# Layer 0 of a three-layer interaction network rebuilt from squared pair sums, with the state copies on ScalarE and the products' tiles in 8 KB packets

## The chip, the cores and the metric

One core of a Trainium2 chip. The metric is the device time of one execution in microseconds, lower is better. Five engines work side by side and wait for one another through semaphores: TensorE (PE; its weight loads are PEld), VectorE (DVE), ScalarE (ACT), GpSimd (POOL) and SyncE (SP), which here only issues transfers. Sixteen DMA engines carry the transfers of all of them.

## The reference

For 1024 samples, 32 embedding rows of 16 numbers are gathered from 32 tables, and three layers of products of pairs follow, each with 64 outputs; the sums over the 16 numbers, with 16 context features, go through a small network.

```python
e = stack([tbl_f[ids[:, f]] for f in range(32)], axis=1)     # B=1024, M=32, D=16
x0 = xk = e
for W in (W0, W1, W2):                                        # W: M x H x 64, H = 32, 64, 64
    xk = relu(einsum('bmd,bhd,mhk->bkd', x0, xk, W))
    outs.append(sum(xk, axis=2))
h = concatenate([concatenate(outs, 1), dense_ctx], 1)         # 208 wide
h = maximum(h @ W_top1 + b_top1, 0)                           # 512
h = maximum(h @ W_top2 + b_top2, 0)                           # 256
y = h @ W_top3
```

Everything is float32. Layer 0 multiplies the embeddings with themselves, so it is symmetric in its two factors: 528 different products of rows. Layers 1 and 2 have 32 x 64 = 2048 products each for every one of the 16384 columns (sample and position).

## The kernel before

The 16384 columns are worked off in 16 **pairs** p of 1024 columns (two chunks of 512, which go to the lower and the upper 64 partitions of an accumulator). For a pair:

- GpSimd gathers 16 x 128 rows of 64 bytes (`gather`, L377) into `gath`, in the order that `stage` copies from the row numbers. SP stores them to a scratch tensor in DRAM (`store_x0`, L251), twice over, so that a row index can wrap.
- SP loads from the scratch what layer 0 needs (`load_x`, L255 to L262): `x_rep`, every row on all four blocks of 32 partitions, `x_rot`, the same rows turned by q + 4u, and `x16`, the turn by 16. Each of these transfers writes 32 partitions.
- SP loads the tiles `m_rep` (`load_m`, L271), 8 tiles of 128 x 1024: block q of tile t holds row 4t + q on all its 32 partitions. Four transfers of 1 MB, each writing 32 partitions. There are three buffers of 8 tiles.
- Layer 0: VectorE multiplies `x_rot` by `x_rep` (`layer0`, 2 units of two tiles, L455) and `x16` (L463); TensorE multiplies by the weights (L662, L674) into `acc0`.
- Layers 1 and 2: ScalarE applies the ReLU while it copies an accumulator four times (`order0`, L560) and eight times (`order1`, L568) into `rep0` and `rep1` (PSUM) and eight times into `xb_pool` (SBUF), and once more into `state` (L555). VectorE makes 6 units a layer (`layer`, L455, a unit is two tiles, `m_rep` times `rep`), GpSimd makes 2 (`products`, L416), of whose last VectorE makes a strip of 112 columns (`edge`). TensorE adds each unit with 4 matmuls of 512 columns (8 instructions, L662).
- VectorE sums each `state` over the 16 positions (`sum_d`, L471).

The order of a pair in the loops, on every engine, is layer 1 of p, layer 0 of p + 1, layer 2 of p - 1. Products go through a ring of 4 buffers (`RING`), with `unit_ready` and `unit_used`. `load_x(p + 2)` waits until VectorE has made layer 0 of p + 1 (`unit_ready`, `p16_ready`). Pair 0 is done in halves ahead of the loops (L508, L704, L582). After the last pair the sums are brought together by 12 transfers and the network at the end runs on TensorE and ScalarE (L760 to L777).

Of the kernel before, what the change touches and what calls it, by code (L numbers as in the profile page):

```python
# [7 lines left out]
U32 = mybir.dt.uint32  # L29
ALU = mybir.AluOpType  # L30
RELU = mybir.ActivationFunctionType.Relu
AX_X = mybir.AxisListType.X
# [6 lines left out]
HC = CHUNK // 2  # L39
NP = B * D // PAIR  # L40
BC = CHUNK // D
GPP = 2 * BC // Q
HG = GPP // 2
LEAD = 4
T = M // Q
DVE_UNITS = 6
POOL_UNITS = 2
RING = 4
M_BUFS = 3
EDGE = 112  # L50
L0_UNITS = 2
PER_ITER = 2 * DVE_UNITS + L0_UNITS
# [4 lines left out]
def build(nc, ids, limits, tables, wa, wb, w1, w2, wt1, bt1, wt2, bt2, wt3, dense, out):  # L57
    ctx = ExitStack()
    with ctx:
# [6 lines left out]
        def sem(name):  # L66
# [3 lines left out]

        x0_dram = nc.dram_tensor("x0_scratch", [NP, 2 * M, PAIR], F32).ap()

# [3 lines left out]
        row_now = [sb(f"row_now{i}", [128, GPP], U32) for i in range(2)]  # L76
        gath = [sb(f"gath{i}", [128, GPP, D]) for i in range(2)]

        x_rep = sb("x_rep", [128, PAIR])
        x_rot = sb("x_rot", [128, 4, PAIR])  # L80
        x16 = sb("x16", [2 * M, 2, CHUNK])

        m_rep = sb("m_rep", [128, M_BUFS * T, PAIR])
        wa_sb = sb("wa_sb", [128, 5, K])
        wb_sb = sb("wb_sb", [128, 4, K])
        w0_sb = sb("w0_sb", [128, 4, K])
# [28 lines left out]
        w0_in = sem("w0_in")  # L115
        w1_in = sem("w1_in")
# [5 lines left out]
        rows_staged = sem("rows_staged")  # L122
# [718 lines left out]
```

## Time and profile before

| | us |
|---|---|
| median of three runs | 773.81 |
| lowest, highest | 772.15, 776.86 |
| span of the profiled execution, first to last instruction | 775.5 |
| busy PE, DVE, POOL, ACT | 593.1, 595.6, 576.2, 408.5 |
| mean granted clock of TensorE | 0.921 of full |
| DMA: bytes, mean rate | 123.07 MB, 159 GB/s |

The page lists no time of the profiled execution other than its span, which lies within the three runs and 1.7 us above their median. Busy times overlap, so they do not add up to the span. No engine is above 77%: who waits for whom has to be read from the waits and from stretches of the timeline. [...]

### The profile page before, as it was taken

To read this page: it belongs to the slowest core of one execution; us is meant where nothing else is said; L and a number is where in the kernel's file an instruction comes from. 1 tells how busy PE (TensorE), PEld (TensorE's weight loads), DVE (VectorE), ACT (ScalarE), POOL (GpSimd) and SP (SyncE) were. 2 spreads that over 40 slices of the span, in tenths; PEclk is the share of its full clock that TensorE was granted. 3 is DMA by queue.
4 is the path that set the end of the run, shared out by engine and by line. 5 is a ranking of instruction groups with operands and counts; after the bars stand their busy time and mean duration, and the time that the engine had idled before them with its cause. 6 is when DMAs were issued, how large, how long until landed. Compare 5 with 4: busy or idle time off the path is not lost.

```text
span 775.5 us, 8340 instructions
## 1 busy us (share of the span) xinstructions
PE 593.1 (76%) x2532; PEld 189.3 (24%) x2532; DVE 595.6 (77%) x325; ACT 408.5 (53%) x724; POOL 576.2 (74%) x340
## 2 busy tenths in 40 slices
PE   0256563998289978969499959769599959799998
PEld 0133111322023222213123212213132212222243
DVE  0143459999399969879799958799899969899910
ACT  0123480867238673746357745727367726657522
POOL 6775679698868889898868888898978887626400
PEclk9968795999779998989799999999899989999999
DMA  3799989794979789797979698897979697990000
GB/s 88 160 195 210 204 180 202 156 206 91 204 147 208 151 170 203 152 205 151 204 150 205 118 201 173 182 199 155 205 152 204 136 207 151 203 197 8 7 8 0
DMA packets 56099, 123.07 MB, mean 159 GB/s; under 512 B 16177, under 2 KB 25265, under 8 KB 56082
## 3 DMA queue, kind: packets, MB, share of 16 engines
q1 hardware_dynamic: 47890, 120.75, 76.8%
q0 software_dynamic: 8192, 2.11, 3.0%
q8 instruction: 8, 0.13, 0.1%
q14 instruction: 9, 0.07, 0.0%
HBM read 117.84 MB, written 4.20 MB: 157 GB/s over the span
## 4 chain that ended last, share of the span: by engine, by line
POOL 27%; DVE 18%; issue 16%; DMA 15%; PE 14%; ACT 5%; SPq 4%; POOLq 0%; DVEq 0%; ACTq 0%
DVE prod L455 16%; POOL gath L377 16%; POOL prod_pool L416 11%; PE acc L662 10%; DMA x<-x_scratch 8%; DMA gath<-in_tables,row_now 4%; ACT rep L568 4%; PE rep L769 2%; DMA x_scratch<-gath 2%; SPq L251 1%; DMA m_rep<-x_scratch 1%; DVE z_sb L471 1%; SPq L258 1%; SPq L255 1%; PE rep L760 1%
## 5 line engine op out<-in xcount | busy, mean ns | idle before, releaser
L662 PE MATMUL acc<-prod,w_sb 128*64 128x512 f32 x1728 | 425.2, 631 | 119.2 <-DVE prod L455 117.9
L455 DVE TENSOR_TENSOR prod<-m_rep,rep 128x2048 f32<-128x2048 f32 x186 | 416.1, 2273 | 17.9 <-DMA m_rep<-x_scratch 10.1
L377 POOL DMA_INDIRECT gath<-in_tables,row_now x256 | 287.1, 1121 | 81.8 <-issue 68.4
L416 POOL TENSOR_TENSOR prod_pool<-m_rep,xb_pool 128x2048 f32<-128x2048 f32 (+1 forms) x62 | 276.7, 4490 | 62.0 <-PE acc L662 54.6
L568 ACT ACTIVATE xb_pool<-acc 32x512 f32<-32x512 f32 x248 | 146.0, 589 | 162.4 <-PE acc L674 157.6
L662 PEld LDWEIGHTS acc<-prod,w_sb 128*64 128x64 f32 x1728 | 124.0, 144 | 407.4 <-issue 230.1
L568 ACT ACTIVATE rep<-acc 32x512 f32<-32x512 f32 x248 | 139.9, 564 | 68.4 <-DVE prod L455 63.4
L455 DVE TENSOR_TENSOR prod<-x_rot,x_rep 128x2048 f32<-128x2048 f32 x30 | 101.9, 3436 | 75.8 <-DMA x<-x_scratch 72.2
L662 PE MATMUL acc<-prod_pool,w_sb 128*64 128x512 f32 x496 | 117.2, 593 | 4.5 <-POOL prod_pool L416 4.5
L560 ACT ACTIVATE rep<-acc 64x512 f32<-64x512 f32 x124 | 70.7, 570 | 51.2 <-DVE prod L455 25.6
L704 PE MATMUL acc<-prod,w_sb 128*64 128x256 f32 x128 | 21.5, 498 | 48.5 <-DVE prod L508 48.4
L662 PEld LDWEIGHTS acc<-prod_pool,w_sb 128*64 128x64 f32 x496 | 35.4, 137 | 76.9 <-issue 71.0
L471 DVE TENSOR_REDUCE z_sb<-state 128x512 f32 (+1 forms) x48 | 32.3, 673 | 6.2 <-ACT state L555 6.2
L555 ACT ACTIVATE state<-acc 128x512 f32<-128x512 f32 x47 | 26.5, 596 | 14.3 <-PE acc L662 13.5
L582 ACT ACTIVATE rep<-acc 32x256 f32<-32x256 f32 (+1 forms) x24 | 8.5, 353 | 47.2 <-PE acc L724 46.9
L508 DVE TENSOR_TENSOR prod<-m_rep,rep 128x2048 f32<-128x2048 f32 x6 | 13.5, 2283 | 20.2 <-DMA m_rep<-x_scratch 18.5
L463 DVE TENSOR_TENSOR prod<-x 64x512 f32<-64x512 f32 x15 | 27.0, 1803 | 0.0
L704 PEld LDWEIGHTS acc<-prod,w_sb 128*64 128x64 f32 x128 | 11.3, 178 | 57.6 <-issue 35.1
L508 DVE TENSOR_TENSOR prod<-x_rot,x_rep 128x2048 f32<-128x2048 f32 x2 | 4.6, 2292 | 25.7 <-DMA x<-x_scratch 25.7
L547 DVE COPY prod<-rep 1x256 f32<-1x256 f32 x2 | 0.8, 422 | 28.2 <-PE rep L777 28.2
L674 PE MATMUL acc<-prod,wa_sb 32*64 32x512 f32 x60 | 16.4, 624 | 6.7 <-DVE prod L463 6.7
L393 POOL TENSOR_TENSOR prod_pool<-m_rep,xb_pool 128x2048 f32<-128x2048 f32 x2 | 9.1, 4537 | 8.3 <-DMA m_rep<-x_scratch 8.2
(29 smaller groups left out, 90.3 us busy)
## 6 DMA issues: line engine op xcount, KB each, us to landing
m_rep<-x_scratch SPq DMA_DIRECT2D x56, 1024.0 KB, 23.3
x_rot<-x_scratch SPq DMA_DIRECT2D x60, 512.0 KB
x_rep<-x_scratch SPq DMA_DIRECT2D x60, 128.0 KB
m_rep<-x_scratch SPq DMA_DIRECT2D x12, 512.0 KB, 21.1
gath<-in_tables,row_now POOLq DMA_INDIRECT x256, 2.4
x_scratch<-gath SPq DMA_DIRECT2D x60, 64.0 KB
x<-x_scratch SPq DMA_DIRECT2D x30, 128.0 KB
x_rot<-x_scratch SPq DMA_DIRECT2D x8, 256.0 KB, 4.5
```

The costliest lines, as they stand in the source:

```text
L377: pool.indirect_dma_start(out=gath[par][:, g, :], out_offset=None, in_=tables, in_offset=bass.IndirectOffsetOnAxis(ap=row_now[par][:, g:g ...
L416: nc.gpsimd.tensor_tensor(prod_pool[:, u, :, 0:hi], m_tiles(p, T - 2 * POOL_UNITS + 2 * u, 2, 0, hi), xb_pool[l - 1][:, None, 0:hi].to_bro ...
L455: nc.vector.tensor_tensor(prod[:, slot, :, :], in0, in1[:, None, :].to_broadcast([128, 2, PAIR]), ALU.mult).then_inc(unit_ready, 1)
L463: nc.vector.tensor_tensor(prod16[:, :], x16[:, 0, :], x16[:, 1, :], ALU.mult).then_inc(p16_ready, 1)
L471: nc.vector.tensor_reduce(out=dst, in_=state[l][:, :].rearrange("k (b d) -> k b d", d=D), op=ALU.add, axis=AX_X).then_inc(z_ready[l], 1)
L508: nc.vector.tensor_tensor(halves(prod[:, n % RING]), in0, in1[:, None, :].to_broadcast([128, T // 2, CHUNK]), ALU.mult).then_inc(unit_read ...
L555: nc.scalar.activation(state[l][:, :], bank[:, :], RELU).then_inc(state_ready[l], 1)
L560: last = nc.scalar.activation(chunk_of(p, rep[0][K * c:K * c + K, :], a), in_chunk(p, acc[l][par][K * a:K * a + K, :]), RELU)
L568: last = nc.scalar.activation(chunk_of(p, dst[M * q:M * q + M, :], a), in_chunk(p, acc[l][par][h:h + M, :]), RELU)
L662: last = nc.tensor.matmul(bank[K * a:K * a + K, :], w, chunk_of(p, tiles[i], a), start=start and i == 0, stop=stop and i == len(ws) - 1)
L674: last = nc.tensor.matmul(acc[0][0][K * a:K * a + K, :], wa_sb[M * a:M * a + M, 4, :], prod16[M * a:M * a + M, :], start=False, stop=True)
L704: last = nc.tensor.matmul(bank[K * a:K * a + K, HC * h:HC * h + HC], w, tiles[:, i, HC * a:HC * a + HC], start=start and i == 0, stop=stop ...
```

## The change

The loops become a list of 32 **slots**, one for each layer 1 or 2 of a pair, written out in full: (1,0), (2,0), (1,1), then (1,p), (2,p-1) for p from 2 to 15, then (2,15).

- **Layer 0 from squares.** 2ab = (a+b)^2 - a^2 - b^2. The weight of a pair of rows is halved, goes on the squared sum, and the weights of the squares are corrected (`wdiag_sb`). For p from 3 on, three of four tiles of sums (`pairs`) are made by transfers: SP copies row m into them (L318), and GpSimd issues a transfer that adds the partner rows (`add_partners`, L366). The fourth is made by TensorE with a 0/1 matrix (`pair_sums`, L655) in PSUM. ScalarE squares them (`square_pairs` L518, `square` L512, `square_x` L502). VectorE has nothing to do for layer 0 any more, save in pair 1. Pairs 0 to 2 use TensorE for more of the sums.
- **ScalarE copies states.** The ReLU is applied once (`relu_state`, L486); `replicate` copies `state` (SBUF) by 8 copies of 32 x 512 to `rep0` and by 8 to `rep1`; `copy_xb` (L535) makes GpSimd's copy by one instruction of 128 x 1024. A state's half v now stands on all four blocks of 32 partitions.
- **Tiles.** Partition 4m + q of tile t holds row m + t, so two tiles come in one packet of 8 KB, and each of a pair's four transfers (L279) writes 128 partitions. Two of them are issued by SP, two by ACT.
- **Units.** 8 units a slot: VectorE makes all 8 in slots 0 to 2, 7 in slots 3 to 27, 6 from slot 28 (L433), GpSimd the rest, each in two halves (`half_unit`, L380) with 4 gathers ahead of each half. In slots of layer 1 GpSimd's last unit is taken by TensorE only after the second unit of the next slot (`late_of`).
- The start: all gathers of pair 0 ahead, layer 0 of pair 0 straight from `gath`. The end: the last product of the network in 32 columns of weights, one transfer for the result.

The core of the diff:

```diff
-                    src = bass.AP(rows.tensor, rows.offset, [[0, M], [Q * PAIR, tiles], [1, PAIR]])
-                    sp.dma_start(dst, src).then_inc(signal, 16)
...
+        def load_tiles(eng, p, js=range(T // 2)):
+            for j in js:
...
+                row = x0_dram[p, 2 * j:2 * j + 1, :]
+                src = bass.AP(row.tensor, row.offset, [[PAIR, M], [0, Q], [1, 2 * PAIR]])
+                eng.dma_start(m_tiles(p, 2 * j, 2), src).then_inc(m_in[p % M_BUFS][j], 16)
...
+                    for n in range(2):
+                        src = bass.AP(row.tensor, row.offset, [[PAIR, M], [0, Q * ADDED[n]], [1, PAIR]])
+                        sp.dma_start(pairs[:, 2 * n:2 * n + ADDED[n], :], src).then_inc(base_in[n], 16)
...
+            def add_partners(p, n):
...
+                pool.wait_ge(base_in[n], 16 * (p - ADDED_FROM + 1))
+                row = x0_dram[p, 1 + 2 * n:2 + 2 * n, :]
+                src = bass.AP(row.tensor, row.offset, [[PAIR, M], [ST * PAIR, Q], [1, ADDED[n] * PAIR]])
+                pool.dma_start(pairs[:, 2 * n:2 * n + ADDED[n], :], src, accum_op=ALU.add).then_inc(pairs_in[n], 16)
...
+            def replicate(i, v, chunks=2):
+                l, p = SLOTS[i]
+                act.wait_ge(state_ready[l - 1], p + 1)
+                for a in range(chunks):
+                    for q in range(Q):
+                        last = nc.scalar.copy(rep[v][M * q:M * q + M, CHUNK * a:CHUNK * a + CHUNK],
+                                              state[l - 1][K * a + M * v:K * a + M * v + M, :])
...
+                for half in range(2):
+                    for a in range(2):
+                        last = nc.tensor.matmul(sums[K * half:K * half + K, CHUNK * a:CHUNK * a + CHUNK],
+                                                sel_of[M * a:M * a + M, K * half:K * half + K],
+                                                x0c[p % 2][M * a:M * a + M, :], start=True, stop=True)
+                    a, rows = half, slice(M * (2 + half), M * (2 + half) + M)
+                    nc.tensor.matmul(acc[K * a:K * a + K, :], diag[rows, :], xsq[rows, :], start=True, stop=False)
...
+            def layer0(p):
...
+                acc = acc_of(0, p)
+                for n in range(2):
+                    pe.wait_ge(pairs_sq, 2 * (p - ADDED_FROM) + n + 1)
+                    for t in range(2 * n, 2 * n + ADDED[n]):
+                        w = half_sb[:, t, :] if t < XT else w0_sb[:, t, :]
+                        last = layer0_tile(acc, w, pairs[:, t, :], False, False)
+                last.then_inc(pairs_read, 1)
+                pe.wait_ge(sq_ready, sums_to(p + 1))
+                layer0_tile(acc, w0_sb[:, ST - 1, :], pairs[:, ST - 1, :], False, True).then_inc(l0_done, 1)
```

TensorE's order, first in the kernel before, at the last pairs, where the loop is written out: layer 0 of pair 15 (L662 from `w_sb`, L674) between layer 1 of pair 14 (`acc_0`) and layer 2 of pair 13.

```order
L662 MATMUL acc_0<-prod,w_sb 64x512 x16
L662 MATMUL acc_0<-prod_pool,w_sb 64x512 x4
L662 MATMUL acc_0<-prod,w_sb 64x512 x4
L662 MATMUL acc_0<-prod_pool,w_sb 64x512 x4
L662 MATMUL acc_0<-prod,w_sb 64x512 x4
L662 MATMUL acc<-prod,w_sb 64x512 x8
L674 MATMUL acc<-prod,wa_sb 64x512 x2
```

The same engine in the changed kernel, two slots in the middle: layer 1 (`acc`), in it the pair sums, behind it layer 0 of the next pair, then layer 2 (`trio`).

```order
L754 MATMUL acc<-prod,w_sb 64x512 x20
L655 MATMUL trio<-x0c,sel_sb 64x512 x2
L659 MATMUL trio<-xsq,wdiag_sb 64x512
L655 MATMUL trio<-x0c,sel_sb 64x512 x2
L659 MATMUL trio<-xsq,wdiag_sb 64x512
L754 MATMUL acc<-prod,w_sb 64x512 x8
L678 MATMUL trio<-pairs,half_sb 64x512 x4
L678 MATMUL trio<-pairs,w_sb 64x512 x4
L754 MATMUL trio<-prod,w_sb 64x512 x8
L754 MATMUL acc<-prod_pool,w_sb 64x512 x4
L754 MATMUL trio<-prod,w_sb 64x512 x20
L754 MATMUL trio<-prod_pool,w_sb 64x512 x4
```

Layer 0 went from 10 matmuls a pair to 14, six of them in the midst of layer 1, and layer 1's GpSimd unit (`acc<-prod_pool`) stands within layer 2's.

ScalarE's order before, for the layers 1 and 0 of one pair in the loop.

```order
L568 ACTIVATE xb_pool<-acc_1 32x512 [waits pool_ready]
L568 ACTIVATE xb_pool<-acc_1 32x512 x7
L560 ACTIVATE rep<-acc_1 64x512 [waits unit_ready]
L560 ACTIVATE rep<-acc_1 64x512 x3
L603 ISA
L604 REGISTER_ALU [waits edge_ready]
L568 ACTIVATE rep<-acc_1 32x512 [waits unit_ready]
L568 ACTIVATE rep<-acc_1 32x512 x7
L161 REGISTER_ALU
L555 ACTIVATE state<-acc_1 128x512 [waits z_ready1]
```

ScalarE's order in the changed kernel, from the second half of the states' copies for a slot of layer 1 to the end of that slot.

```order
L525 COPY rep<-state 32x512 [waits state_ready0,unit_ready]
L525 COPY rep<-state 32x512 x7
L486 ACTIVATE state<-trio 128x512 [waits z_ready2,pool_used,unit_used]
L525 COPY rep<-state 32x512 [waits state_ready1,unit_ready]
L525 COPY rep<-state 32x512 x7
L535 COPY xb<-rep 128x1024 [waits pool_ready,rep0_ready]
L518 ACTIVATE pairs<-pairs 128x2048 [waits pairs_in0]
L518 ACTIVATE pairs<-pairs 128x1024 [waits pairs_in1]
L512 ACTIVATE pairs<-trio 128x1024 [waits l0_done,sums_ready]
```

The eight copies to `xb` are gone; the three squares of the next pair's layer 0 stand behind the copy of `rep0`, and ahead of the next slot's copies to `rep1`.

## Rows read from the trace of the kernel before

**Rows 1.** The page: span, busy time and share of each engine, instructions.
```profile
span 775.5 us, 8340 instructions
PE 593.1 (76%) x2532; PEld 189.3 (24%) x2532; DVE 595.6 (77%) x325; ACT 408.5 (53%) x724; POOL 576.2 (74%) x340
```

**Rows 2.** Waits: engine, line, waited for: us in total, times, longest.
```profile
ACT xb_pool L568 <- PE acc L674: 157.6, 14, 25.2
...
DVE prod L455 <- DMA x<-x_scratch: 72.2, 10, 11.6
```

**Rows 3.** Stretches: us; busy PE, PEld, DVE, ACT, POOL (instructions); clock; DMA share; GB/s.
```profile
396.00:442.00 46.00, 44.51 (x204) 13.87 (x202) 45.38 (x27) 33.29 (x59) 36.56 (x20) 1.00 0.82 162
...
488.00:534.00 46.00, 36.16 (x156) 10.62 (x154) 40.34 (x22) 24.80 (x45) 40.89 (x23) 0.96 0.92 182
...
5.00:7.00 2.00, 0.00 (x0) 0.00 (x0) 0.20 (x1) 0.00 (x0) 1.39 (x3) 1.00 0.98 382
...
680.00:690.00 10.00, 9.91 (x38) 2.58 (x36) 10.00 (x7) 5.11 (x9) 0.00 (x0) 0.83 1.04 204
```

**Rows 4.** Timeline of SP, the tiles' loads of the second and the fifteenth pair.
```profile
146.80 2.00 SPq L271 DMA_DIRECT2D m_rep<-x_scratch  x4
...
660.22 1.82 SPq L271 DMA_DIRECT2D m_rep<-x_scratch  x4
```

**Rows 5.** Timeline of DVE: start, us, what, in brackets the idle time before.
```profile
143.15 8.86 DVE L455 TENSOR_TENSOR prod<-m_rep,rep 128x2048 f32<-128x2048 f32 x4
151.94 0.67 DVE L471 TENSOR_REDUCE z_sb<-state 128x512 f32 x1
152.54 2.27 DVE L455 TENSOR_TENSOR prod<-m_rep,rep 128x2048 f32<-128x2048 f32 x1
...
461.93 4.49 DVE L455 TENSOR_TENSOR prod<-x_rot,x_rep 128x2048 f32<-128x2048 f32 x2 [9.15 <-DMA x<-x_scratch]
```

**Rows 6.** Timeline of PE within one pair, at full clock.
```profile
425.25 1.07 PE L674 MATMUL acc<-prod,wa_sb 32*64 32x512 f32 x4
426.26 3.65 PE L662 MATMUL acc<-prod,w_sb 128*64 128x512 f32 x16
...
434.53 1.89 PE L662 MATMUL acc<-prod_pool,w_sb 128*64 128x512 f32 x8
436.25 1.89 PE L662 MATMUL acc<-prod,w_sb 128*64 128x512 f32 x8
```

**Rows 7.** Groups of the page: count, busy us, mean ns of one, idle before.
```profile
L568 ACT ACTIVATE xb_pool<-acc 32x512 f32<-32x512 f32 x248 | 146.0, 589 | 162.4 <-PE acc L674 157.6
...
L455 DVE TENSOR_TENSOR prod<-x_rot,x_rep 128x2048 f32<-128x2048 f32 x30 | 101.9, 3436 | 75.8 <-DMA x<-x_scratch 72.2
...
L555 ACT ACTIVATE state<-acc 128x512 f32<-128x512 f32 x47 | 26.5, 596 | 14.3 <-PE acc L662 13.5
L582 ACT ACTIVATE rep<-acc 32x256 f32<-32x256 f32 (+1 forms) x24 | 8.5, 353 | 47.2 <-PE acc L724 46.9
```

**Rows 8.** Timeline of POOL within one pair.
```profile
426.67 8.59 POOL L416 TENSOR_TENSOR prod_pool<-m_rep,xb_pool 128x2048 f32<-128x2048 f32 x2
...
436.71 0.95 POOL L377 DMA_INDIRECT gath<-in_tables,row_now  x1 [0.30 <-issue]
```

**Rows 9.** The start: first and last gather of pair 0, the gathers' landing, first tiles multiplied.
```profile
4.07 1.15 POOL L377 DMA_INDIRECT gath<-in_tables,row_now  x1 [0.28 <-POOL row_now L372]
...
23.03 0.95 POOL L377 DMA_INDIRECT gath<-in_tables,row_now  x1 [0.30 <-issue]
...
44.16 4.48 DVE L508 TENSOR_TENSOR prod<-m_rep,rep 128x2048 f32<-128x2048 f32 x2 [13.46 <-DMA m_rep<-x_scratch]
...
gath<-in_tables,row_now POOLq DMA_INDIRECT x256, 2.4
```

**Rows 10.** The end on PE: last unit of layer 2, first matmul of the network.
```profile
741.44 1.89 PE L662 MATMUL acc<-prod,w_sb 128*64 128x512 f32 x8
743.26 1.12 PE L760 MATMUL rep<-x_rot 128*128 128x512 f32 x2
```

More of the change, by code:

```diff
@@ L212, in halves @@
[L212 to L231 removed]
+            if count > 0:
+                eng.wait_ge(s, count)
@@ L438, in _, with gather @@
-            pairs(pool, body, 2, NP - 4)
+            def gather(first, count):
+                for n in range(first, min(first + count, NP * GPP)):
+                    p, g = n // GPP, n % GPP
+                    if g == 0:
+                        after(pool, x0_stored, 32 * (p - 1))
+                        if p in (3, 4):
+                            pool.wait_ge(x0c_in[p % 2], 16 * Q)
+                    pool.indirect_dma_start(
+                        out=gath[p % 2][:, g, :], out_offset=None, in_=tables,
+                        in_offset=bass.IndirectOffsetOnAxis(ap=rows_sb[:, n:n + 1], axis=0),
+                    ).then_inc(first_gathered if n < WARM_FROM else gathered[p % 2], 16)
@@ new lines, in _ @@
+            for i in range(POOL_FROM, NS):
+                l, p = SLOTS[i]
+                if l == 1 and p + 1 < NP:
+                    for n in range(2):
+                        add_partners(p + 1, n)
+                if i == POOL_FROM:
+                    first = (POOL_FROM + 2) * GPP - 2 * BURST
+                    gather(ahead, first - ahead)
+                    ahead = first
+                for k in range(pool_units(i)):
+                    for j in range(2):
+                        gather(ahead, BURST)
+                        ahead += BURST
+                        half_unit(i, k, j)
@@ L637, in _ @@
+            relu_slot(NS - 1)
             act.wait_ge(top_in, 7 * 16)
@@ L651, in _ @@
             act.wait_ge(top_ready, g + 1)
[L652 to L654 removed]
+            nc.scalar.copy(y_sb, top[0][:, 0:B // Q]).then_inc(y_ready, 1)
         @block.tensor
         def _(pe):
[L658 to L665 removed]
@@ new lines, in unit @@
+            def unit(acc, src, ws, start, stop, used, number=None):
+                for k, w in enumerate(ws):
+                    if k == 1 and number is not None:
+                        pe.wait_ge(unit_ready, number + 1)
+                    for a in range(2):
+                        last = nc.tensor.matmul(acc[K * a:K * a + K, :], w, src[:, k, CHUNK * a:CHUNK * a + CHUNK],
+                                                start=start and k == 0, stop=stop and k == 1)
+                last.then_inc(used, 1)
```

997 lines of the change are left out of this document (500 added, 497 removed).

## The prediction

> **What bounds the kernel now.** I read the page's busy shares first [rows 1]: no engine is above 77%, so the time is lost in waits. The list of waits says where [rows 2]: VectorE stands 72.2 us for the loads of layer 0's operands, and ScalarE 157.6 us for layer 0's last matmul. The issues of the tiles' loads give the pace: from the second to the fifteenth pair 660.22 - 146.80 = 513.4 us for 12 pairs, 42.8 us a pair [rows 4]. What VectorE has to do in a pair is less. Four units start to end in 151.94 - 143.15 = 8.79, 2.20 us each, and a sum takes 0.60 [rows 5], so 12 units, the 3 sums, two units of layer 0 at 2.20 and some 1.4 for the small ones are 34. The rest is waiting, and one wait is in the same view: 9.15 us ahead of `x_rot` times `x_rep` [rows 5]. The reason is a chain around the DMA engines. Layer 0's operands (2.75 MB) may only be loaded when those of the pair before are used up, the tiles (4 MB) queue behind them, and both go at 204 GB/s with the engines full [rows 3]: 6.75 MB are 33 us, and stores and landings come on top. In the stretch in which the wait is absent, VectorE is busy 45.38 of 46 us and TensorE 44.51 [rows 3]: these two are next. In a usual stretch TensorE is busy 36.16 [rows 3].
>
> **The change part by part.** Prices first, all from stretches without waits.
> TensorE: 8 instructions (a unit) every 436.25 - 434.53 = 1.72 us, 0.215 each at full clock; four with 32 rows of weights 426.26 - 425.25 = 1.01 us, 0.25 each [rows 6]. ScalarE: 0.589 for 32x512, 0.596 for 128x512, 0.353 for 256 columns [rows 7], so 0.24 for each further 256 columns and about 0.12 fixed: 1.1 for 1024, 2.0 for 2048 columns. GpSimd: 8.59 / 2 = 4.3 a unit; a gather every 0.95 + 0.30 = 1.25 us [rows 8].
>
> *VectorE, a pair from slot 3 on.* Off go two units and a small product of layer 0 (3436 ns mean, longer than 2.2 wherever GpSimd reads beside them [rows 7]) and the strip. On come 14 units instead of 12: 14 x 2.20 + 3 x 0.60 = 32.6 us.
>
> *TensorE.* 14 + 2 units x 1.72 = 27.5. Layer 0: 8 full matmuls are 16 instructions x 0.215 = 3.4, 6 with 32 rows are 12 x 0.25 = 3.0. Sum 33.9 us, a little above VectorE. So TensorE is next, at a pace that the densest stretch bounds better than the bare pitch: 204 instructions in 46 us, 0.2255 each with its gaps, clock 1.00 [rows 3]. A pair has 156 instructions: 35.2 us. In the first half of a double slot it falls behind by layer 0's 28 instructions (6.4 us) and in the second it catches up: 9 units x 1.72 = 15.5 against VectorE's 16. The ring of four (8.8 us) carries that; with 4 us of ordinary lag the oldest buffer comes free just in time, so I count no stall of VectorE for it.
> [...]
>
> *ScalarE.* A pair: 32 copies x 0.589 = 18.8, 3 ReLU x 0.6 = 1.8, two of 1024 columns for GpSimd 2.2, squares 2.0 + 1.1 + 1.1 + 0.6 = 4.8, two issues of tiles about 1: 28.6 of 35. What matters is its order. In a slot of layer 1 the first 3 units and a sum end at 7.2 us; then 8 copies (4.7) and GpSimd's copy (1.1) end at 13.0, the squares at 17.2, the slot at 16.6. The next slot's 8 copies to `rep1` end at 21.9, and are needed at 16.6 + 6.6 + 0.6 = 23.8. Slack: 1.9 us. So it is hidden, if the added pairs have landed by 13.0.
>
> *Added pairs.* The trace shows no adding transfer. From below, 1.5 MB go as a plain load at the best rate seen, 382 GB/s (weights, 128 partitions [rows 3]): 3.9 us. From above, at 204 GB/s and twice over, since the destination is read too: 14.7 us. SP's base copy may start when layer 0 of the pair before is through (some 6 us into the slot of layer 2) and lands at about 13; GpSimd has little to do by then and issues the adding ones 3 us before the slot of layer 1. That leaves 16 us, so both ends fit and I take zero. GpSimd: 16 x 1.25 + 2 x 4.3 + two issues of about 1 = 30.6 of 35, and its late unit is taken 9 us into the next slot: hidden.
>
> *Loads.* 4 + 1.5 + 1.5 + 0.4 = 7.4 MB a pair. At 204 GB/s this is 36.3 us and would be a bound of its own; at 382 it is 19.4. The kernel before writes 32 partitions with each transfer of scratch data and gets 204; its two weight loads write 128 and get 382. The new ones all write 128, except the small `x0c`. I take 382.
> [...]
>
> *The start.* Sixteen gathers from 4.07, the last issued at 24, landed 2.4 later [rows 9]: 26.4. Sums on TensorE, squares, layer 0, ReLU and copies by TensorE are an estimate from the prices above: 2 for 32 short matmuls' instructions, 4 x 1.1 squares, 1.5 for 8 matmuls, 0.6, and 2 for the copies, 10.5 us: first product at 37; its tiles, stored and loaded meanwhile, are there at 35. Before, tiles were first multiplied at 44.16. Slot 0: 8 x 2.20 = 17.6; 3.3 for the last half unit, ReLU and copy; slot 1: 17.6 + 2.2 + 0.6 = 20.4; slot 2: 18.8; 2.7 until layer 0 of pair 2 has gone through ReLU and both copies. Slot 3 begins at 99.8. The gathers of pair 2 end at 75 to 80, ahead of their use.
>
> *The body.* From slot 3 TensorE has 199 units of VectorE and 33 of GpSimd, 232 x 8 = 1856 instructions, and 13 x 28 = 364 for layer 0: 2220 x 0.2255 = 500.6. With 2.2 for the first product: 602.6.
>
> *The end.* From the last layer-2 matmul to the end of the span 775.5 - 743.3 = 32.2 [rows 1, 10], during which TensorE is nearly always at work; I leave it, as the new last product saves under 1. Sum 634.8. The span before lies 1.7 above the median: 633.
>
> **The rivals.** A: *an operand comes late every pair.* If the adding transfers land after 13.0 + 1.9 us, each us more delays `rep1` and VectorE. For: two landings in a row, and nothing in the trace shows their speed. Against: 16 us of room. 3 us too late in 13 pairs: 39, that is 672.
> B: *the pair sums do not run side by side.* Two of them share their columns of the array and differ only in rows; in the kernel before paired matmuls differ in columns. If those 8 instructions take double, 0.25 x 8 = 2.0 more a pair, 26 in 13 pairs, that is 659.
> C: *the scratch stays at 204 GB/s*, because it is the source that is slow. 36.3 instead of 35.2 a pair, and landings late in addition, about 2.5: 13 x 2.5 = 33, that is 666. Against it stands 382 for weights, which lie in DRAM too.
> D: *slower than before.* The adding transfers go packet by packet at a price near that of the gathers, where 128 rows of 64 bytes take 2.4 us to land [rows 9]; with 4 or 8 KB a row and an addition that could be tens of us. ScalarE's queue holds the copies of `rep1` behind the squares, so all stops. The gain to eat up is 141 us in 13 pairs, 10.8 each: it decides when the larger one lands later than 13.0 + 1.9 + 10.8 = 25.7 us into the slot, 29 after its issue, or under 36 GB/s. At 40 us after issue: 633 + 13 x 22 = 919 at worst; at 31, 800.
> E: *TensorE keeps its bare pitch*, 2220 x 0.215 = 477 instead of 501: 610.
>
> **How the numbers follow.** Forecast 633 with its own range 618 to 655 (start and each slot's handover give 10 either way, gaps of one more us a pair 15): 0.62. A 0.13, B 0.09, C 0.04, E 0.08, D 0.03, and 0.01 for no change, if two of A to C come together at three times the size. The range 8 in 10: from 612 to 672. A measurement tells about 1% from no change. Faster by over 1%: 0.62 + 0.13 + 0.09 + 0.04 + 0.08 = 0.96, within 1% 0.01, slower 0.03.
>
> **What would show it.** Right: no wait of VectorE for layer 0's operand; TensorE busy over 95% between 110 and 590 us with clock 1.0; tiles landing in under 10 us; DMA share near 0.5 to 0.6 with peaks near 380 GB/s; `rep1` never the last to come; slots in pairs of 34 to 36 us; first product at 37, slot 3 at 100. Wrong: ScalarE idle ahead of L518 (A, D); L655 rows of over 2.5 us for 8 instructions (B); stretches at 204 GB/s with share 1 (C); a clock below 1.0 in the body, which would mean that TensorE waits.

## The result, and the profile after

| | before | changed |
|---|---|---|
| median (lowest to highest) | 773.15 (772.15 to 776.86), 4 runs | 624.13 (620.18 to 625.63), 4 runs |
| span of the profiled execution | 775.5 | 618.4 |

The ratio is 0.8052, 95% interval 0.8017 to 0.8086. The page of the changed kernel, beside [rows 1]: span, busy times, and the DMA queues with packets, MB and their share of 16 engines' span (q1 is SP's, q10 ScalarE's, q0 GpSimd's with gathers and adding transfers).

```profile
span 618.4 us, 7354 instructions
...
PE 573.8 (93%) x2658; PEld 184.2 (30%) x2658; DVE 523.7 (85%) x280; ACT 409.7 (66%) x630; POOL 438.7 (71%) x364
...
q1 hardware_dynamic: 24372, 69.88, 31.1%
q0 software_dynamic: 11936, 22.56, 20.8%
q10 hardware_dynamic: 5028, 29.40, 12.4%
```

VectorE's and GpSimd's busy times fell by 72 and 138 us. The queues tell the rate while packets are under way: q10 29.40 MB / (0.124 x 618.4 us) = 383 GB/s, q1 363, and q0 only 175. The waits of the changed kernel, beside [rows 2] (engine, line, waited for: us, times, longest):

```profile
ACT xsq L502 <- DMA x0c<-x_scratch: 59.8, 12, 9.1
DVE prod L433 <- PE rep L745: 35.6, 3, 26.7
...
PE acc L754 <- DVE prod L433: 14.5, 30, 1.7
...
DVE prod L433 <- ACT rep L525: 6.9, 7, 1.9
```

VectorE's 72.2 us for layer 0's operands are gone. What is left on it is at the start: 35.6 us are the wait for the first product (26.7) and two handovers. TensorE waits for VectorE's products. The longest wait, 59.8 us of ScalarE for the small `x0c`, could be moved away without any gain, as a run below shows. Stretches of the changed kernel, beside [rows 3] (us; busy PE, PEld, DVE, ACT, POOL; clock; DMA share; GB/s):

```profile
110.00:590.00 480.00, 467.28 (x2228) 148.60 (x2229) 463.83 (x244) 375.35 (x580) 363.30 (x280) 1.00 0.71 214
290.00:500.00 210.00, 208.29 (x1012) 66.32 (x1012) 210.00 (x110) 174.45 (x267) 172.18 (x139) 1.00 0.78 240
...
314.00:318.00 4.00, 4.00 (x22) 1.33 (x20) 4.00 (x3) 3.90 (x8) 3.06 (x4) 1.00 0.93 190
334.00:340.00 6.00, 6.00 (x30) 2.01 (x28) 6.00 (x3) 5.44 (x11) 4.93 (x5) 1.00 0.99 401
```

From 290 to 500 VectorE is busy 210 us of 210: nothing holds it up, its own list is the time. TensorE's 208.29 looks the same but isn't, since ends of matmuls are modelled and it waits for products in the list above; a run below takes work from it. While tiles land (334 to 340) the engines move 401 GB/s at a share of 0.99, while adding transfers are under way (314 to 318) 190 at 0.93.

ScalarE's squares (L518) mark a pair each. In the timeline of ACT in the changed kernel:

```profile
122.32 1.91 ACT L518 ACTIVATE pairs<-pairs 128x2048 f32<-128x2048 f32 x1 [0.33 <-DMA pairs<-x_scratch]
...
293.78 2.86 ACT L518 ACTIVATE pairs<-pairs 128x2048 f32<-128x2048 f32 x2
...
456.38 2.86 ACT L518 ACTIVATE pairs<-pairs 128x2048 f32<-128x2048 f32 x2
```

456.38 - 293.78 = 162.60 us for five pairs, 32.52 a pair, where [rows 4] gave 42.8. Thirteen pairs times 10.3 are 134 of the 157 us between the two spans; of the other 23 the first product, 7.4 us earlier, is a third. The first four pairs behind 122.32 are slower than that: 37.6, 34.0, 33.0 and 34.6.

The timeline of PE in one pair, beside [rows 6]:

```profile
326.68 0.64 PE L655 MATMUL trio<-x0c,sel_sb 32*64 32x512 f32 x2
...
327.19 0.59 PE L659 MATMUL trio<-xsq,wdiag_sb 32*64 32x512 f32 x1
327.71 3.65 PE L754 MATMUL acc<-prod,w_sb 128*64 128x512 f32 x16
331.19 1.89 PE L678 MATMUL trio<-pairs,half_sb 128*64 128x512 f32 x8
...
334.62 3.60 PE L754 MATMUL trio<-prod,w_sb 128*64 128x512 f32 x16
```

From the first 32-row matmul to the next full one are 327.71 - 326.68 = 1.03 us for 12 instructions, 0.086 each. They go in two passes: six start within 0.04 us at 326.68 and six more at 327.16 (the rows merge neighbours of one line). The full ones keep their pitch, (334.62 - 331.19) / 16 = 0.214.

The timeline of DVE at the start, and one uninterrupted row of the body:

```profile
36.73 6.68 DVE L433 TENSOR_TENSOR prod<-m_rep,rep 128x2048 f32<-128x2048 f32 x3 [26.70 <-PE rep L745]
...
58.38 11.08 DVE L433 TENSOR_TENSOR prod<-m_rep,rep 128x2048 f32<-128x2048 f32 x5 [3.32 <-PE rep L745]
...
83.80 4.48 DVE L433 TENSOR_TENSOR prod<-m_rep,rep 128x2048 f32<-128x2048 f32 x2 [5.55 <-PE rep L745]
...
108.92 4.49 DVE L433 TENSOR_TENSOR prod<-m_rep,rep 128x2048 f32<-128x2048 f32 x2 [6.26 <-ACT xb L535]
...
318.09 22.05 DVE L433 TENSOR_TENSOR prod<-m_rep,rep 128x2048 f32<-128x2048 f32 x10
```

The first product is at 36.73 (44.16 in [rows 9]). Slots 2 and 3 begin with waits of 5.55 and 6.26 us. TensorE's timeline just ahead of the second:

```profile
101.39 1.89 PE L678 MATMUL trio<-prod_pool,half_sb 128*64 128x512 f32 x8
103.11 1.89 PE L678 MATMUL trio<-prod_pool,w_sb 128*64 128x512 f32 x8
104.83 1.89 PE L754 MATMUL acc<-prod,w_sb 128*64 128x512 f32 x8
106.64 1.13 PE L745 MATMUL rep<-state,xb 64*128 64x512 f32 x4
```

VectorE's slot 2 ended at 102.7. Layer 0 of pair 2 stands in TensorE's queue in front of the slot's last two units and ends at 104.83; the ReLU follows at 105.04; the copy by TensorE (L745) is queued behind a unit of 1.81 us, so that it begins at 106.64; `xb` is copied at 107.87. In slot 1 it is the same: layer 0 of pair 1 until 80.81, a unit, the copy at 82.62.

The end, beside [rows 10]:

```profile
586.65 1.12 PE L831 MATMUL rep<-m_rep 128*128 128x512 f32 x2
```

618.4 - 586.65 = 31.75 us remain, much as before (32.2).

Landings of the changed kernel (KB each, median us from issue to landing):

```profile
m_rep<-x_scratch SPq DMA_DIRECT2D x38, 1024.0 KB, 11.1
m_rep<-x_scratch ACTq DMA_DIRECT2D x26, 1024.0 KB, 7.5
...
pairs<-x_scratch POOLq DMA_DIRECT2D x13, 1024.0 KB, 9.5
...
pairs<-x_scratch POOLq DMA_DIRECT2D x13, 512.0 KB, 13.2
```

### The profile page after: what moved, and what is told of

Same layout as the page of the kernel before. It is cut to its first block, busy times and chain, and to the rows that moved or that the text cites. A ratio compares the mean times of both kernels' runs of the same rounds, so it can differ in the third digit from the quotient of the medians.

```text
span 618.4 us, 7354 instructions
## 1 busy us (share of the span) xinstructions
PE 573.8 (93%) x2658; PEld 184.2 (30%) x2658; DVE 523.7 (85%) x280; ACT 409.7 (66%) x630; POOL 438.7 (71%) x364
## 3 DMA queue, kind: packets, MB, share of 16 engines
q0 software_dynamic: 11936, 22.56, 20.8%
q10 hardware_dynamic: 5028, 29.40, 12.4%
## 4 chain that ended last, share of the span: by engine, by line
PE 51%; DVE 16%; POOL 15%; issue 13%; DMA 3%; ACT 1%; SPq 0%; ACTq 0%; DVEq 0%; POOLq 0%
PE trio L754 21%; PE acc L754 19%; DVE prod L433 15%; POOL gath L356 12%; PE trio L678 5%; PE rep L839 2%; DVE z_sb L443 2%; POOL prod_pool L380 2%; PE trio L655 1%; POOL unread L395 1%; PE rep L831 1%; PE rep L832 1%; DMA pairs<-x_scratch 1%; DMA gath<-in_tables,rows_sb 1%; DMA x_scratch<-gath 1%
## 5 line engine op out<-in xcount | busy, mean ns | idle before, releaser
L433 DVE TENSOR_TENSOR prod<-m_rep,rep 128x2048 f32<-128x2048 f32 x222 | 492.5, 2277 | 48.8 <-PE rep L745 35.6
L356 POOL DMA_INDIRECT gath<-in_tables,rows_sb x256 | 247.8, 968 | 80.4 <-issue 69.8
L525 ACT COPY rep<-state 32x512 f32<-32x512 f32 x472 | 274.1, 581 | 22.4 <-DVE prod L433 16.0
L754 PE MATMUL acc<-prod,w_sb 128*64 128x512 f32 x904 | 207.5, 598 | 14.6 <-DVE prod L433 14.5
L754 PE MATMUL trio<-prod,w_sb 128*64 128x512 f32 x880 | 197.1, 596 | 4.4 <-DVE prod L433 4.3
L380 POOL TENSOR_TENSOR prod_pool<-m_rep,xb 128x1024 f32<-128x1024 f32 x66 | 157.4, 2398 | 26.7 <-PE acc L754 13.4
L754 PEld LDWEIGHTS acc<-prod,w_sb 128*64 128x64 f32 x904 | 60.0, 136 | 158.2 <-issue 93.5
L754 PEld LDWEIGHTS trio<-prod,w_sb 128*64 128x64 f32 x880 | 62.8, 137 | 132.3 <-issue 116.7
L502 ACT ACTIVATE xsq<-x0c 64x512 f32<-64x512 f32 x15 | 9.4, 628 | 59.8 <-DMA x0c<-x_scratch 59.8
L366 POOL DMA_DIRECT2D pairs<-x_scratch x26 | 25.1, 980 | 31.5 <-DMA pairs<-x_scratch 31.0
L518 ACT ACTIVATE pairs<-pairs 128x2048 f32<-128x2048 f32 (+1 forms) x26 | 37.6, 1479 | 4.4 <-DMA pairs<-x_scratch 4.2
L486 ACT ACTIVATE state<-acc 128x512 f32<-128x512 f32 x17 | 10.2, 598 | 37.8 <-PE acc L754 22.6
L486 ACT ACTIVATE state<-trio 128x512 f32<-128x512 f32 x31 | 18.3, 589 | 22.2 <-PE trio L754 13.1
L535 ACT COPY xb<-rep 128x1024 f32<-128x1024 f32 x29 | 29.4, 1014 | 3.1 <-PE rep L745 2.2
L754 PE MATMUL acc<-prod_pool,w_sb 128*64 128x512 f32 x120 | 28.3, 592 | 0.0
L754 PEld LDWEIGHTS trio<-prod_pool,w_sb 128*64 128x64 f32 x144 | 10.3, 137 | 23.3 <-issue 20.0
L655 PE MATMUL trio<-x0c,sel_sb 32*64 32x512 f32 x120 | 16.4, 613 | 0.0
L512 ACT ACTIVATE pairs<-trio 128x1024 f32<-128x1024 f32 x15 | 15.1, 1007 | 1.6 <-PE trio L641 1.6
## 6 DMA issues: line engine op xcount, KB each, us to landing
m_rep<-x_scratch SPq DMA_DIRECT2D x38, 1024.0 KB, 11.1
pairs<-x_scratch POOLq DMA_DIRECT2D x13, 512.0 KB, 13.2
```

The source lines that it names most:

```text
L356: pool.indirect_dma_start(out=gath[p % 2][:, g, :], out_offset=None, in_=tables, in_offset=bass.IndirectOffsetOnAxis(ap=rows_sb[:, n:n + 1 ...
L366: pool.dma_start(pairs[:, 2 * n:2 * n + ADDED[n], :], src, accum_op=ALU.add).then_inc(pairs_in[n], 16)
L380: nc.gpsimd.tensor_tensor(prod_pool[:, at % POOL_RING, j], m_tiles(SLOTS[i][1], t, 1)[:, 0], xb[i % 2][:, :], ALU.mult).then_inc(pool_read ...
L433: nc.vector.tensor_tensor(prod[:, number % RING], in0, in1[:, None, :].to_broadcast([128, 2, PAIR]), ALU.mult).then_inc(unit_ready, 1)
L486: nc.scalar.activation(state[l][:, :], acc_of(l, p), RELU).then_inc(state_ready[l], 1)
L518: nc.scalar.activation(tiles, tiles, SQUARE).then_inc(pairs_sq, 1)
```

## The experiments

Three questions were open: what sets 32.5 us a pair, what makes the tiles land faster, and what the adding transfers cost. The runs came in four groups at different times, on three chips. In three of them the kernel before took 785 us where it took 773 above, while the changed kernel hardly differed (626). So ratios to the kernel before in the same group are compared: those of the three groups with that of the changed kernel repeated in one of them, 0.7967 (0.7932 to 0.8002), and those of the group of x0c_first, where the kernel before took 773, with 0.8052.

### Who sets the pace: TensorE, VectorE, or both

TensorE less: two of the four tiles of layer 0 from pair 3 on, 8 instructions or 1.7 us a pair, are left out.

```diff
-                    for t in range(2 * n, 2 * n + ADDED[n]):
+                    for t in range(2 * n, 2 * n + n):
```

> Leaves out two of the four tiles of layer 0 on TensorE from pair 3 on: 4 matmuls, 8 instructions, 1.72 us a pair, 22 us in 13 pairs. Theory V (VectorE sets the pace at 14 x 2.20 + 3 x 0.60 = 32.6 us a pair, TensorE has 32.0): no more than 3 us less. Theory T (TensorE sets the pace, as I predicted): 15 to 22 us less.

VectorE less: the sums over 16 positions read 2 of them. Over the 48 sums VectorE's busy time falls from 523.7 to 502.8 us, 0.44 each or 1.3 a pair.

```diff
-                nc.vector.tensor_reduce(out=z_sb[l][:, p, :], in_=state[l][:, :].rearrange("k (b d) -> k b d", d=D),
+                nc.vector.tensor_reduce(out=z_sb[l][:, p, :], in_=state[l][:, :].rearrange("k (b d) -> k b d", d=D)[:, :, 0:2],
```

> Each of VectorE's 48 sums reads 2 of the 16 positions instead of all (the rest of the sum is left out), some 0.45 us less each, 1.35 a pair. Theory V: the pair falls from 32.55 to TensorE's 32.0, then TensorE is next: 5 to 9 us less. Theory T: no change, within 2 us.

Both edits together:

> The two cuts together (two tiles of layer 0 left out, sums over 2 of 16 positions). Theory V: a pair falls by all of VectorE's 1.35, as TensorE is now at 30.3: 17 to 22 us less, more than the sum of the two alone. Theory T: as TensorE alone, 15 to 22, so this run tells by its sum with the others: under V the single cuts give little and the pair of them much.

| | median us | ratio (95%) |
|---|---|---|
| changed kernel, repeated | 626.46 | 0.7967 (0.7932 to 0.8002) |
| TensorE less | 626.84 | 0.7950 (0.7914 to 0.7986) |
| VectorE less | 627.34 | 0.7992 (0.7957 to 0.8027) |
| both less | 621.79 | 0.7893 (0.7842 to 0.7945) |

TensorE has room: 22 us of its work went and nothing came of it, where 15 to 22 us had to come if it set the pace. In that kernel ACT's L518 rows at 177.92 and 373.29 are six pairs apart, 32.56 each, the pace of the changed kernel. Taking work from VectorE alone gave nothing either, against the 5 to 9 us that were expected. Taking it from both gave 4.7 us in the medians (0.9% by the ratios, with intervals that overlap), against 17 to 22. So it isn't a race of two. The waits of the kernel with less on VectorE:

```profile
ACT xsq L502 <- DMA x0c<-x_scratch: 58.5, 12, 6.8
...
DVE prod L433 <- ACT rep L525: 18.5, 16, 2.3
```

VectorE's waits for ScalarE's copies are 18.5 us here, 6.9 in the changed kernel and 1.9 in its repeat. The pace of this kernel was 32.8 (ACT's L518 rows at 200.64 and 463.28, eight pairs), no faster than with all of VectorE's work. So in the changed kernel VectorE's list sets the pace, and something else stands within a few tenths of a microsecond behind it. These waits say that it is ScalarE's chain: 27.0 us busy a pair (174.45 / 210 x 32.52), 59.8 / 12 = 5.0 at each wait for `x0c`, and `rep1` in the order behind all of that. This is argued from the waits. Whether ScalarE's work, the load of `x0c` or the added pairs hold this chain was not separated.

### Is ScalarE's wait for `x0c` a cost?

The square of `x0c` made later in ScalarE's order, behind the next slot's copies:

```diff
-                    if i == 3:
-                        square_x(nxt)
-                    else:
+                    square_x(nxt)
+                    if i > 3:
                         relu_slot(i - 1)
...
-                if i > 3 and l == 2 and p + 3 < NP:
-                    square_x(p + 3)
```

> ScalarE squares x0c (square_x, whose load it waits for 59.8 us in all) behind the copies to rep1 of the next slot instead of ahead of them and of a ReLU. Theory L (in the first pairs the pace is set by a loop: layer 0's last matmul, base copies and x0c load, ScalarE's wait, rep1, VectorE): the waits of 1.87, 1.24, 0.41, 0.35, 0.64 us of VectorE for ScalarE's copies go, pairs 4 to 8 come down from 34 towards 32.6, in all 3 to 7 us less than the changed kernel. Rival (the added pairs set the early pace): within 1.5 us of it, with VectorE's or ScalarE's wait moved to pairs_in.

Measured 626.29 us, ratio 0.7974 (0.7950 to 0.7999): no difference to 0.7967. The wait of L502 is gone from the list, and others stand for it:

```profile
ACT rep L525 <- DVE prod L433: 63.7, 30, 3.7
...
ACT pairs L518 <- DMA pairs<-x_scratch: 10.1, 12, 1.8
...
DVE prod L433 <- ACT rep L525: 3.6, 4, 1.2
```

ScalarE is through earlier and waits all the longer for VectorE, 63.7 us instead of 16.0. The wait of 59.8 us, the longest of all for a load, was worth nothing here, because the engine that bounds was busy during it. What the run can't tell is the price of VectorE's own 6.9 us of waiting for the copies, which the expectation counted on: in the repeated changed kernel they were 1.9 us already, and are 3.6 here.

The other way round, `x0c` issued by SP ahead of the pairs' base copies, so that it comes early (the same lines are taken out behind them):

```diff
...
                 elif p >= ADDED_FROM:
+                    sp.wait_ge(l0_done, p - 1)
+                    for a in range(2):
+                        sp.dma_start(x0c[p % 2][M * a:M * a + M, :],
+                                     x0_dram[p, 0:M, CHUNK * a:CHUNK * a + CHUNK]).then_inc(x0c_in[p % 2], 16)
```

> SP issues the small loads of x0c (128 KB) ahead of the base copies (1.5 MB) instead of behind them. ScalarE waits 59.8 us in all for x0c, and behind that wait stand its copies to rep1, for which VectorE waits 1.87, 1.24, 0.41, 0.35 and 0.64 us in pairs 4 to 7. Theory: these waits go, 3 to 5 us less. Rival (in the early pairs the store and the gathers are late, not the queue): x0c lands at most 2 us earlier and the base copies later, within 1.5 us of no change.

And with this GpSimd's twice-used units begin at slot 26 instead of 28 (`POOL_TWICE = 26`):

> As x0c_first, and GpSimd makes two units from slot 26 on instead of 28, since its gathers end there: VectorE has two units, 4.4 us, less. If VectorE alone sets the pace: 4 us less than x0c_first. If TensorE is only 0.5 us a pair behind it, as counted: 0 to 1.5 us less.

Measured 625.61 us, ratio 0.8105 (0.8071 to 0.8138), and 625.10, 0.8091 (0.8066 to 0.8115), beside 0.8052 (0.8017 to 0.8086): neither is faster. Both ratios are 0.5 to 0.7% higher, with intervals that overlap, so a loss isn't shown either. The expected 3 to 5 us didn't come; the rival on record, no change, did. Waits and landings of the first:

```profile
ACT pairs L517 <- DMA pairs<-x_scratch: 22.2, 25, 3.0
...
ACT xsq L501 <- DMA x0c<-x_scratch: 13.1, 12, 3.9
...
DVE prod L432 <- ACT rep L524: 11.6, 13, 2.7
```

```profile
pairs<-x_scratch POOLq DMA_DIRECT2D x13, 1024.0 KB, 12.9
```

The wait for `x0c` fell from 59.8 to 13.1 us, the adding transfers landed at 12.9 instead of 9.5, and now it is their wait that stands ahead of `rep1`. The wait was moved, not removed. GpSimd's two units more, which take 4.4 us from VectorE's list, gave nothing measurable either. No version that still computes the whole result was faster than the changed kernel.

### GpSimd's last unit in its own slot

```diff
-    return i >= POOL_FROM and SLOTS[i][0] == 1 and SLOTS[i][1] + 1 < NP
+    return False
```

> Undoes the late use: in slots of layer 1 TensorE takes GpSimd's last unit at the end of its own slot. In the steady stretch that unit is ready at 328.7 and TensorE would come to it at 331.2, so theory H (late use only matters in the first pairs, where GpSimd is behind): 0 to 6 us more, all of it ahead of 240 us of the trace. Theory W (late use is what hides GpSimd in every pair): over 13 us more, 1 us and more in each pair.

Measured 635.65 us, ratio 0.8035 (0.7974 to 0.8095) against 0.7967: 0.8% or some 5 us more, with intervals that overlap a little. The trace takes the same side. VectorE now waits for buffers of the ring:

```profile
DVE prod L433 <- PE trio L754: 5.9, 11, 2.1
...
DVE prod L433 <- PE acc L754: 4.4, 3, 2.4
```

and ACT's L518 rows at 172.50 and 404.30, seven pairs, are 33.1 us apart instead of 32.5. Over all twelve pairs from the first L518 row to the last it is 398.8 us against 392.6 in the repeated changed kernel, 0.5 a pair. So this part of the change is worth about 0.5 us in every pair, some 3 to 5% of the whole gain, as far as these runs tell. Both theories on record miss this: the sum is that of the first, but it is not all in the first pairs.

### What makes the tiles land faster

The same 8 KB packets, but each transfer split by partitions, into four of 32 (shown) or two of 64; the count waited for grows with them:

```diff
-                row = x0_dram[p, 2 * j:2 * j + 1, :]
-                src = bass.AP(row.tensor, row.offset, [[PAIR, M], [0, Q], [1, 2 * PAIR]])
-                eng.dma_start(m_tiles(p, 2 * j, 2), src).then_inc(m_in[p % M_BUFS][j], 16)
+                for h in range(4):
+                    row = x0_dram[p, 2 * j + M // 4 * h:2 * j + M // 4 * h + 1, :]
+                    src = bass.AP(row.tensor, row.offset, [[PAIR, M // 4], [0, Q], [1, 2 * PAIR]])
+                    eng.dma_start(m_tiles(p, 2 * j, 2)[128 // 4 * h:128 // 4 * (h + 1)], src).then_inc(m_in[p % M_BUFS][j], 16)
```

> The same tiles in 8 KB packets, but each transfer cut into four that write 32 neighbouring partitions, as every transfer of scratch data did in the kernel before. Theory P (the partitions that a transfer writes set its rate): the tiles fall back to about 204 GB/s, 4 MB take 19.6 us a pair, with 4.1 for the base copies, 8.6 for the added ones and 1.5 for the rest 34 us, over VectorE's 32.6: 635 to 680 us. Theory K (the packets' size sets it): no change, 622 to 627.

> Each tile transfer cut in two halves of 64 neighbouring partitions. [...] Rival (the count of partitions alone): a rate of about 300 and no loss. Theory K: no change.

And 128 partitions with packets of 4 KB, one tile a transfer:

> Each tile by itself, 128 partitions, packets of 4 KB, 8 transfers a pair instead of 4. Theory P: the rate stays (packets of 4 KB in about half the time of those of 8 KB), the time within 3 us of the changed kernel; the issues cost SP and ACT 0.6 us each more. Theory K: the tiles at about 204 GB/s, 635 us and more.

| | median us | ratio (95%) | tiles of q10 |
|---|---|---|---|
| 128 partitions, 8 KB | 626.46 | 0.7967 | 383 GB/s |
| 128 partitions, 4 KB | 635.81 | scatters from 627 to 645, no interval | 364 |
| 64 partitions, 8 KB | 690.54 | 0.8785 (0.8738 to 0.8831) | 238 |
| 32 partitions, 8 KB | 736.49 | 0.9326 (0.9262 to 0.9391) | see below |

The rates are the queue's bytes, 2 MB of weights among them, over its share of the span; 383 is from the first trace of the changed kernel, and its repeat gives 392. For 4 KB and for 64 partitions (spans 631.6 and 686.5 us):

```profile
q10 hardware_dynamic: 8772, 29.40, 12.8%
```

```profile
q10 hardware_dynamic: 5444, 29.40, 18.0%
```

Packets of half the size cost 5 to 7% of the rate, and this run also issues twice as many transfers, as the one with 64 partitions does. The time of the 4 KB kernel can't be told within its scatter. Half the partitions with packets of the same size take the rate from 383 to 238 and bring back 0.082 x 785 = 64 us of the 160 that the change gains there. The pace is 38.0 us a pair (L519 rows of ACT at 211.86 and 439.99, six pairs). A stretch of this kernel:

```profile
290.00:324.00 34.00, 29.19 (x128) 8.97 (x126) 27.66 (x16) 23.25 (x39) 22.13 (x19) 0.95 0.89 219
```

VectorE is busy 27.66 of 34 us and the DMA share is at 0.89. From this kernel's list of waits:

```profile
ACT xsq L503 <- DMA x0c<-x_scratch: 121.2, 12, 11.8
...
DVE z_sb L444 <- ACT state L487: 41.7, 12, 5.0
...
DVE prod L434 <- ACT rep L526: 30.2, 15, 3.1
```

The slower tiles delay the transfers behind them, ScalarE waits for `x0c` with the ReLU and the copies behind it, its slack is used up, and the delay arrives at VectorE, which waits for the state and for `rep`. Of the theories on record for this run, the packets' size (no change) and the count of partitions alone (some 300 GB/s and no loss) fall. The measured 238 GB/s is nearer to the 204 of the kernel before, whose transfers write 32 partitions, than to 383.

That 32 partitions cost still more (107 us, 736 where 635 to 680 were expected) doesn't measure the partitions alone. A stretch of that kernel:

```profile
374.00:378.00 4.00, 0.00 (x0) 0.00 (x0) 0.61 (x1) 0.00 (x0) 1.01 (x1) 0.87 0.52 193
```

Compute all but stands still from 374 to 378, and yet only half of the DMA time is used; by its share q10 moved 356 GB/s. The single packets in the traces show more. The tiles' packets of 8 KB on q10 take 0.31 us each (median from 150 us on) in the changed kernel, most often with 16 under way at a time. With 64 partitions it is 16 as well, but 0.57 us each. With 32 partitions they take 0.31 again, but hardly ever more than 8 are under way. So in that kernel the tiles' packets weren't slow, but only half as many were under way, as the share of 0.52 of the sixteen engines says too. The slowest dimension of such a transfer's source is 8 here, 16 with 64 partitions and 32 in the changed kernel; these three kernels have most often 8, 16 and 16 packets under way. What sets their number no run tested beyond that. The run with 64 partitions has as many under way as the changed kernel, so it is the clean one for the partitions. The packets of 4 KB fit it: 0.33 us each in the kernel before, to 32 partitions, and 0.16 on q10 of the 4 KB kernel, to 128 (medians from 150 us on), most often with 16 under way in both.

### The adding transfers

GpSimd's transfers copy the partner rows instead of adding them:

```diff
-                pool.dma_start(pairs[:, 2 * n:2 * n + ADDED[n], :], src, accum_op=ALU.add).then_inc(pairs_in[n], 16)
+                pool.dma_start(pairs[:, 2 * n:2 * n + ADDED[n], :], src).then_inc(pairs_in[n], 16)
```

> The partner rows are written over the base rows instead of added to them (layer 0 then squares the partner alone from pair 3 on). Theory: adding costs a transfer about half its rate (22.56 MB of GpSimd's queue at 175 GB/s beside 363 and 383 on the others), which is hidden from pair 8 on: the queue's share falls from 20.8% to some 12%, landings of 9.5 and 13.2 us fall to 6 to 8, and the time by 0 to 5 us, all in the first pairs. Rival (the added pairs are what VectorE's small waits of the early pairs come from and more): 8 us and more.

Measured 623.89 us, ratio 0.7934 (0.7882 to 0.7986) against 0.7967: 2.6 us less in the medians (626.46 against 623.89), not told apart from none. The pace is 32.55 from the second pair on. The queue (span of 622.3 us):

```profile
q0 software_dynamic: 11936, 22.56, 12.3%
```

It takes 12.3% of the engines' time instead of 20.8 for the same bytes: the addition costs 0.208 x 618.4 - 0.123 x 622.3 = 52 us of all sixteen engines over 13 pairs, 4.0 a pair for 1.5 MB, about what the bytes themselves cost. The queue's 8 KB packets take 0.63 us with the addition and 0.31 without (medians). It is almost all hidden.

## Why the prediction was right, and where its sum was off

The forecast was 633 (span 634.8), measured 624.13 (span 618.4), within its own range. The engine that the forecast named as the one that sets the pace, TensorE, was the wrong one: it is VectorE. By its steps:

- **What bounds the kernel before: right.** With operands that don't wait for the loads the waits went, and slowing the tiles' loads alone took back 64 us. No run undoes the squares of layer 0 alone, so their share of the gain is argued from the waits that are gone. The pace of 42.8 us holds: the two rows of [rows 4] are twelve loads apart, although they are called the second and the fifteenth pair.
- **First product at 37: right**, 36.73. Slot 1 was to begin at 57.9 and began at 58.38.
- **Slots 1 to 3: short by 9.1 us.** The handover from slot 1 to 2 was counted at nothing and took 5.55; that from 2 to 3 was counted at 2.7 and took 6.26. The step left out that TensorE's copy of the state is queued behind a unit, and that layer 0 ends 2 to 3 us behind VectorE. Slot 3 began at 108.92 instead of 99.8.
- **TensorE's price of a pair: the mis-sized term.** "6 with 32 rows are 12 x 0.25 = 3.0" measured 1.03. [rows 6] has two such matmuls side by side, in two passes of some 0.5 us; here six stand side by side in two passes of some 0.5 us. The price is that of a pass, the same for two and for six, and it was multiplied by the instructions. With it TensorE needs 27.5 + 3.4 + 1.0 = 32.0 us, below VectorE's 32.6, and the factor of 0.2255 an instruction was taken for the wrong engine. Rival B, that these don't run side by side, was the wrong way round altogether. The body from slot 3 to the last unit took 586.65 - 108.92 = 477.7 us instead of 502.8, 25 less.
- **VectorE's price: right.** 32.6 was worked out, 32.52 measured, and it is this engine that bounds. The mean of 3436 ns for `x_rot` times `x_rep` in the kernel before comes from five of the 30: the median is 2284, and the three longest, 10.8 to 11.2 us, stand beside GpSimd's products for 8.5 us each. Rival E gave 610 for the bare pitch of TensorE; its 477 us for the body are what was measured, but by chance, since VectorE set it.
- **Changes between full and 32-row matmuls: small.** The sum has no term for them. From the start of one pass to that of the next the trace has 0.43 us between full ones, 0.53 from a full to a short one, 0.48 between the two short ones and 0.55 back to a full one (medians from 290 to 500 us). So a change costs some 0.1 us, 0.2 a pair, and the trace has nothing larger for it.
- **ScalarE hidden, slack 1.9 us: right as a whole, thin as said.** VectorE waited 6.9 us for `rep1` over the whole run, in 7 places, where it was said to be never the last to come. In the two kernels with less work on VectorE these waits are the ones that grow.
- **Added pairs at no cost: right.** Landings of 9.5 and 13.2 us lie inside the bounds of 3.9 and 14.7, and the room of 16 held. They do run at half the rate (packets of 0.63 us, 0.31 without the addition), the factor of two of the upper bound, and leaving the addition out gained 2.6 us, within the scatter. Rivals A and D did not come.
- **Loads at 382 GB/s: right**, 383 and 363. The choice of 382 against 204 rested on what the transfers of the kernel before write, 128 and 32 partitions. The runs bear it out: the rate went from 383 to 238 with 64 partitions, and to 364 with packets of 4 KB. Why fewer partitions are slower no run shows. Rival C (the source is slow) fell; its sign, a stretch near 204 GB/s with the engines full, does appear (314 to 318), but there the transfers are the adding ones. DMA share was said to be 0.5 to 0.6 and was 0.71 to 0.78, since the adding transfers weren't in it at their price: 19.4 + 4.0 us of 32.5 are 0.72. Tiles landed in 11.1 and 7.5 us, not all under 10.
- **The end:** 32.2 against 31.75.
- **The signs.** TensorE was busy 467.28 of 480 us with the clock at 1.00, as said for the case that it sets the pace, and yet it didn't: this sign doesn't tell a bound from an engine close behind it. The pairs took 32.5, not 34 to 36.

So the sum is 634.8 + 9.1 - 25.1 - 0.4 = 618.4: a large error and a smaller one of the other sign. That the forecast came as near as 1.4% is partly luck. With the body alone as measured the span would have come out at 609.7, and with the handovers alone at 643.9.

**Open.** The first pairs vary from run to run. The first L518 row of ACT stood at 122.32 in the changed kernel and twelve pairs took 399.1 us from there; in its repeat it stood at 129.81 and they took 392.6, so that they come to the last one at 521 and 522. In the first trace TensorE waits there for GpSimd's unit and ScalarE for `x0c`, with VectorE's operands behind both:

```profile
147.17 1.94 PE L754 MATMUL trio<-prod_pool,w_sb 128*64 128x512 f32 x8 [2.44 <-POOL prod_pool L380]
147.21 0.63 ACT L502 ACTIVATE xsq<-x0c 64x512 f32<-64x512 f32 x1 [9.13 <-DMA x0c<-x_scratch]
```

From 113 to 147 us the chain that ended last goes through GpSimd alone, its gathers and units. So a start that is earlier by a few microseconds may be lost to GpSimd again; this was not tested. In other traces (here the kernel with less on both) VectorE stands before slot 2 for something outside it, and TensorE behind that for nothing that the profile shows:

```profile
88.84 4.49 DVE L433 TENSOR_TENSOR prod<-m_rep,rep 128x2048 f32<-128x2048 f32 x2 [9.52 <-remote]
...
91.27 3.68 PE L754 MATMUL acc<-prod,w_sb 128*64 128x512 f32 x8 [4.75 <-issue]
```

The code before pair 3 differs from pair to pair and is written out; that its instructions came late is the author's guess, which no run tested. Nor was it tried to square `x0c` later together with less work on TensorE and VectorE, which would show whether ScalarE's place in the order or its busy time is what stops those. Nor was the copy from `state` tried alone against the copies from the accumulator, or layer 0 from squares alone.

## What to carry to other kernels

Before a wait in the list is attacked, ask what the bounding engine does meanwhile: 59.8 us of waiting were worth nothing here, and 1.7 us a pair taken from an engine that was 93% busy neither. Ask it anew in each kernel, though: with slower tiles the same wait, 121.2 us long, did reach VectorE. When several limits lie within a microsecond a pair of each other, a single cut may pay nothing: here each of two gave none, and both together less than 1%. Count short matmuls that stand side by side by passes and not by instructions: 12 took 1.03 us here, and 4 took 1.01. Let each transfer write all 128 partitions, which gave 383 GB/s where 64 gave 238; the size of the packets between 4 and 8 KB made 5 to 7% of the rate beside it. Look at how many packets are under way: with 8 in the slowest dimension of the source it was hardly ever more than 8, and the kernel took 736 us instead of 626.

## What the runs showed of the hardware

- Six matmuls with 32 rows and 64 columns of weights, on four row blocks and both column halves, ran side by side: 12 instructions of 512 columns in 1.03 us, 0.086 each, where full ones take 0.214. The two matmuls of [rows 6], side by side as well, take the same two passes for 4 instructions, 0.25 each.
- A change between full and 32-row matmuls and back made the passes start 0.10 and 0.12 us later than among full ones (0.53 and 0.55 against 0.43).
- An adding transfer occupies the DMA engines much longer than a plain one of the same bytes: the queue runs at 175 GB/s with it and at 22.56 MB / (0.123 x 622.3 us) = 295 without; its 8 KB packets take 0.63 and 0.31 us.
- Tiles to 64 partitions went at 238 GB/s and to 128 at 383, both most often with 16 packets of 8 KB under way (0.57 and 0.31 us each). Split by 32 partitions, with a slowest dimension of 8 in the source, the packets took 0.31 us, but hardly ever more than 8 were under way.
- TensorE's granted clock was 1.00 of full from 110 to 590 us, where in the kernel before it was 0.92 over the same stretch. In the kernel with 32 partitions it was 0.50 in the 4 us behind a stretch without a matmul:

```profile
378.00:382.00 4.00, 1.57 (x4) 0.53 (x6) 1.59 (x2) 2.80 (x5) 2.74 (x3) 0.50 0.99 222
```
